# A gated attention and expert block: the operands of TensorE's turns declared float32r

## The reference

```python
def _L0_xattn_ref(p, k_v, W_k, b_k, ln_gamma, ln_beta):
    kv = k_v @ W_k.T + b_k
    out = jnp.einsum('bij,bjd->bid', p, kv)
    sim = jnp.einsum('bid,bjd->bij', out, kv) * scale
    # layer norm of sim over its last axis, with gamma and beta
    attn = jax.nn.softmax(sim, axis=-1)

def _L0_ffn_ref(x, gate_w, e_bias, Wu, Wd, Wsu, Wsd):
    logits = h @ gate_w
    scores = jax.nn.sigmoid(logits)
    # the 4 best of 32 experts, out of the 2 best of 4 groups; weights normalised, times 2.5
    up = jnp.einsum('th,ehi->tei', h, Wu)
    act = _relu2(up)
    routed = jnp.einsum('tei,te,eih->th', act, combine, Wd)
    shared = _relu2(h @ Wsu) @ Wsd
    out = (routed + shared).reshape(orig_shape)

x = x + jnp.tanh(g_xattn[0]) * _L0_xattn_ref(_layernorm(x), ctx_512, ...)
x = x + jnp.tanh(g_ffn[0]) * _L0_ffn_ref(_layernorm(x), ...)
```

## Time and profile before

| | us |
|---|---|
| median of 3 runs | 545.59 (545.41 to 546.27) |
| span of the profiled execution | 543.3 |
| TensorE busy with products and turns | 531.8, 98% of the span |
| weight loads busy | 434.4, 80% |
| VectorE busy | 412.1, 76% |
| ScalarE busy | 339.5, 62% |
| GpSimd busy | 190.0, 35% |

### The profile page before, as it was taken

One profiled execution on the slowest core, in us unless ns is written; L12 is line 12 of the kernel. 1 busy time (PEld: TensorE's weight loads), 2 busy tenths in 40 slices (PEclk: granted clock), 3 DMA queues, 4 the chain that ended last, 5 costly groups with the idle time before them and its releaser, 6 DMA issues.

```text
span 543.3 us, 11125 instructions
## 1 busy us (share of the span) xinstructions
PE 531.8 (98%) x3090; PEld 434.4 (80%) x3091; DVE 412.1 (76%) x906; ACT 339.5 (62%) x669; POOL 190.0 (35%) x194
## 2 busy tenths in 40 slices
PE   7999999999999999999999999999999999999997
PEld 4555776778788888999999999999999999986553
DVE  4799995494998958666787897777677575756997
ACT  4778673755327855677778787776777776753210
POOL 2110000000000032655657766666656566531000
PEclk9999999999999999999999999999999999999999
DMA  8931012006000024997887988788889778899998
GB/s 311 350 125 39 14 65 77 2 1 210 23 1 0 2 78 151 358 322 222 307 254 237 317 274 254 277 261 275 269 299 316 272 246 268 270 316 358 411 415 328
DMA packets 56393, 116.48 MB, mean 214 GB/s; under 512 B 5493, under 2 KB 24054, under 8 KB 55926
## 3 DMA queue, kind: packets, MB, share of 16 engines
q1 hardware_dynamic: 43200, 72.97, 40.8%
q0 software_dynamic: 12960, 42.48, 21.5%
q10 hardware_dynamic: 150, 0.07, 0.0%
HBM read 85.87 MB, written 29.62 MB: 213 GB/s over the span
## 4 chain that ended last, share of the span: by engine, by line
PE 73%; DVE 14%; DMA 5%; ACT 4%; issue 2%; SPq 1%; DVEq 0%; POOL 0%; ACTq 0%; POOLq 0%
PE U L1805 32%; PE D L1805 28%; PE T L2164 6%; DVE X L1782 5%; PE D L2183 3%; DMA yg<-y_rows 2%; PE T L1805 2%; SPq L508 1%; DVE X L1130 1%; DVE X L1184 1%; DMA y_rows<-yb,idx_s 1%; DVE bst L1135 1%; DMA h_rows<-HR 1%; DVE PS L1118 1%; PE T L1963 1%
## 5 line engine op out<-in xcount | busy, mean ns | idle before, releaser
L618 POOL DMA_INDIRECT xg<-h_rows,idx_g x81 | 88.0, 1086 | 107.9 <-DVE idx_g L1530 70.9
L625 POOL DMA_INDIRECT y_rows<-yb,idx_s x81 | 89.6, 1106 | 81.5 <-ACT yb L935 63.9
L1564 DVE TENSOR_TENSOR xgT_lo<-T,xgT_hi 128x512 fp32r<-128x512 f32 x81 | 56.0, 691 | 48.5 <-ACT xgT_hi L918 48.2
L935 ACT ACTIVATE yb<-D 128x512 f32<-128x512 f32 x81 | 48.7, 602 | 58.2 <-PE D L1805 58.2
L1805 PE MATMUL U<-wu_hi,xgT_hi 128*128 x324 | 58.2, 301 | 0.6 <-DVE xgT_lo L1564 0.6
L1805 PE MATMUL D<-wd_hi,eaT_hi 128*128 x162 | 57.3, 435 | 0.0
L918 ACT ACTIVATE xgT_hi<-T 128x512 fp32r<-128x512 f32 x81 | 48.1, 594 | 10.5 <-issue 8.7
L1805 PE MATMUL U<-wu_hi,xgT_lo 128*128 x324 | 51.8, 282 | 0.0
L1805 PE MATMUL U<-wu_lo,xgT_hi 128*128 x324 | 51.6, 281 | 0.0
L1805 PE MATMUL D<-wd_lo,eaT_hi 128*128 x162 | 50.6, 394 | 0.0
L1805 PE MATMUL D<-wd_hi,eaT_lo 128*128 x162 | 50.1, 391 | 0.0
(11 more groups left out here) (272 smaller groups left out, 1131.5 us busy)
## 6 DMA issues: line engine op xcount, KB each, us to landing
wu<-in_L_ffn_Wu SPq DMA_DIRECT2D x32, 512.0 KB, 5.0
wd<-in_L_ffn_Wd SPq DMA_DIRECT2D x32, 512.0 KB, 5.3
yg<-y_rows SPq DMA_DIRECT2D x18, 512.0 KB, 10.9
out<-X SPq DMA_DIRECT2D x16, 256.0 KB, 5.9
X<-in_x SPq DMA_DIRECT2D x3, 1024.0 KB, 11.4
h_rows<-HR SPq DMA_DIRECT2D x3, 1024.0 KB, 4.3
yg<-y_rows SPq DMA_DIRECT2D x3, 1024.0 KB, 12.2
wsu<-in_L_ffn_Wsu SPq DMA_DIRECT2D x2, 1024.0 KB, 8.7
```

The lines of the kernel that those rows point to most:

```text
L618: pool.indirect_dma_start(out=xg[:, u, :], out_offset=None, in_=h_dram[:, :], in_offset=bass.IndirectOffsetOnAxis(ap=idx_g[:, t:t + 1], ax ...
L625: pool.indirect_dma_start(out=y_dram[:, :], in_=yb[:, u, :], in_offset=None, out_offset=bass.IndirectOffsetOnAxis(ap=idx_s[:, t:t + 1], ax ...
L935: ac.activation(yb[:, t % UNROLL, :], D[2 + t % 2][:, :], ACT.Copy)\
L1564: ve.tensor_tensor(xgT_lo[:, t % 2, :, :], T[t % 2][:, :].rearrange("p (h n) -> p h n", h=HB), xgT_hi[:, t % 2, :, :].bitcast(f32), ALU.su ...
```

## The change

All turns of context rows, keys, X, HR, logits, gathered rows and activations read their data through a second name of the same bytes, declared float32r; the output in PSUM is written through a float32r view of the same bank, and the identity is a float32r copy of the old one. The second names are tiles that are allocated and freed just before the old one, so that both get the same address. GpSimd copies the identity, and TensorE waits for this copy once, ahead of its first turn. The turns of the key weights, the bias, the table of experts and the first positions stay fp32. No other instruction changes. The diff, with the other renamed tiles (`HR_r`, `lgT_r`, `key2_r`, `ctx_r`, `keyT_r`, `eact_r`) left out, which follow the pattern of `X_r` and `xg_r`:

```diff
+        with ExitStack() as turned:
+            X_r = turned.enter_context(nc.sbuf_tensor("X_r", [P, NT, H], f32r))
         X = sb("X", [P, NT, H])
...
         ident = sb("ident", [P, P])
+        ident_r = sb("ident_r", [P, P], f32r)
...
+            with ExitStack() as turned:
+                xg_r = at("xg_r", [P, UNROLL, H], turned, f32r)
             xg = at("xg", [P, UNROLL, H], early)
...
+        def keys_turned(b):
+            return key2_r[:, b, :] if b < 2 else keyT_r[:, :]
...
+            pool.wait_ge(s["pool_c"], 2)
+            pool.tensor_copy(ident_r[:, :], ident[:, :]).then_inc(s["pool_i"], 1)
             pool.memset(lower[:, :], 0.0).then_inc(c, 1)
...
             pe.wait_ge(s["pool_c"], 2)
+            pe.wait_ge(s["pool_i"], 1)
             pe.transpose(T[0][:, 0:DC], wk[:, :], ident[:, :]).then_inc(s["pe_wk"], 1)
...
+            def turn(o, bits):
+
+                return pe.transpose(o.bitcast(f32r), bits, ident_r[:, :])
...
-                    i_ = pe.transpose(ctx_bank(b)[:, j * P:(j + 1) * P], ctx_b[:, j, :], ident[:, :])
+                    i_ = turn(ctx_bank(b)[:, j * P:(j + 1) * P], ctx_r[:, j, :])
...
-                    i_ = pe.transpose(T[0][:, j * P:(j + 1) * P], keys_of(b)[:, j * P:(j + 1) * P], ident[:, :])
+                    i_ = turn(T[0][:, j * P:(j + 1) * P], keys_turned(b)[:, j * P:(j + 1) * P])
...
-                    pe.transpose(p_bank(0, j)[:, 0:P], X[:, 0, j * P:(j + 1) * P], ident[:, :])
+                    turn(p_bank(0, j)[:, 0:P], X_r[:, 0, j * P:(j + 1) * P])
...
-                    i_ = pe.transpose(p_bank(b, j)[:, it * P:(it + 1) * P], X[:, b * TPB + it, j * P:(j + 1) * P],
-                                      ident[:, :])
+                    i_ = turn(p_bank(b, j)[:, it * P:(it + 1) * P], X_r[:, b * TPB + it, j * P:(j + 1) * P])
...
-                    i_ = pe.transpose(h_bank(b, it)[:, h * P:(h + 1) * P], HR[:, it, h * P:(h + 1) * P], ident[:, :])
+                    i_ = turn(h_bank(b, it)[:, h * P:(h + 1) * P], HR_r[:, it, h * P:(h + 1) * P])
...
-                    i_ = pe.transpose(U[1][:, it * P:(it + 1) * P], lgT[:, it * P:(it + 1) * P], ident[:, :])
+                    i_ = turn(U[1][:, it * P:(it + 1) * P], lgT_r[:, it * P:(it + 1) * P])
...
-                    i_ = pe.transpose(T[t % 2][:, h * P:(h + 1) * P], xg[:, t % UNROLL, h * P:(h + 1) * P], ident[:, :])
+                    i_ = turn(T[t % 2][:, h * P:(h + 1) * P], xg_r[:, t % UNROLL, h * P:(h + 1) * P])
...
-                    i_ = pe.transpose(D[t % 2][:, k * P:(k + 1) * P], eact[:, t % 2, k * P:(k + 1) * P], ident[:, :])
+                    i_ = turn(D[t % 2][:, k * P:(k + 1) * P], eact_r[:, t % 2, k * P:(k + 1) * P])
```

More of the change, by code:

```diff
@@ L59, in block_kernel @@
             HR_lo = turned.enter_context(nc.sbuf_tensor("HR_lo", [P, TPB, H], f32r))
+        with ExitStack() as turned:
+            HR_r = turned.enter_context(nc.sbuf_tensor("HR_r", [P, TPB, H], f32r))
         HR = sb("HR", [P, TPB, H])
@@ L67, in block_kernel @@
             wsu_h4 = chosen_all.enter_context(nc.sbuf_tensor("wsu_h4", [P, 2, HB, P], f32r))
+        with ExitStack() as turned:
+            lgT_r = turned.enter_context(nc.sbuf_tensor("lgT_r", [P, SEQ], f32r))
         lgT = sb("lgT", [P, SEQ])
@@ L126, in block_kernel @@
                 out2 = at("out2", [DC, 2, SEQ], ramp)
+                with ExitStack() as turned:
+                    key2_r = at("key2_r", [DC, 2, SEQ], turned, f32r)
                 key2 = at("key2", [DC, 2, SEQ], ramp)
@@ L141, in block_kernel @@
             with ExitStack() as attention:
+                with ExitStack() as turned:
+                    ctx_r = at("ctx_r", [P, TPB, DC], turned, f32r)
                 ctx_b = at("ctx_b", [P, TPB, DC], attention)
                 ctxT = at("ctxT", [DC, SEQ], attention)
+                with ExitStack() as turned:
+                    keyT_r = at("keyT_r", [DC, SEQ], turned, f32r)
                 keyT = at("keyT", [DC, SEQ], attention)
@@ L215, in block_kernel @@
             erel = at("erel", [P, 2, INNER], early)
+            with ExitStack() as turned:
+                eact_r = at("eact_r", [P, 2, INNER], turned, f32r)
             eact = at("eact", [P, 2, INNER], early)
@@ L306, in block_kernel @@
         names = """d_x00 d_small d_gate d_tanh d_wk d_bk d_h d_out
-            pool_c pool_r dve_c dve_wh pe_bk pe_g act_bk act_th
+            pool_c pool_i pool_r dve_c dve_wh pe_bk pe_g act_bk act_th
             dve_v dve_u dve_z dve_e dve_x1 dve_h dve_ws dve_lo dve_sh dve_hT dve_lg dve_ch
```

## The result

| | before | after |
|---|---|---|
| median of 4 runs, same chip | 545.55 (545.41 to 546.27) | 539.16 (538.74 to 539.82) |
| ratio | | 0.9887 (0.9875 to 0.99) |
| span of the profiled execution | 543.3 | 536.9 |

The change makes the kernel 6.4 us faster, 1.2%. The direction was as forecast and the time lies in the range, but the forecast was 21.1 us.

A forecast was written before the change was run, and what follows sets the result against it. TensorE, gapless in the expert loop and nearly always busy from 60 to 200 us, was taken as the bound; 18.0 + 3.1 = 21.1 us off the 545.59 us median gave 524.5, range 512 to 546.5.

The forecast's parts named there:

- The identity sets the turn's pace: Each turn on TensorE: the moving fp32 identity costs two cycles a column; float32r brings the stream from 107 to 53 ns.
- Rival 1: Turns cost the same in float32r because all 32 bits are handed on; 545.6 us, chance 0.27.
- The load stays at 140: Weight load of each turn: remains 140 ns in float32r, not a product's 188, since the turn sets it, not the type.
- Rival 2: Slower: float32r turns load in 188 ns and stand 120 apart; 6.3 us lost, 551.9 us, chance 0.16.
- What is late next: Once the stream is short, the turn's load sets the distance: 72 ns from start to start in place of 109.
- The sum for the loop: Expert loop: 486 turns, each cheaper by 109 - 72 ns, all on TensorE's path, gain 18.0 us.
- wrong in its size: Sign of failure: the first products after the turns start later by what the turns gave; no size put on it.
- 60 to 200 us, 3.1: Stretch before the loop: 84 turns gain 37 ns each, 3.1 us taken whole, bounds 0 and 4.5.
- First 60 us: Start of the kernel: 92 turns, other chains set part of the pace, gain taken as 0, at most 4.9 us.
- Tail 0, new copy and wait hidden: Tail has no turns, cost 0; identity's copy on GpSimd and TensorE's wait hidden with 1.8 us to spare, else 0.3.
- Rival 3: Expert loop: turns get cheap but TensorE runs into VectorE or a transfer, giving back half; 535 us, chance 0.07.

The follow-up runs named there:

- r5: A probe kernel of its own, computing nothing of the reference: rows and groups of turns and products on TensorE; float32r turns 86 ns apart, fp32 109; no kernel time.
- r9: Changed kernel with only the first batch's turns in float32r, all others fp32; 547.11 us, ratio 1.004 to the kernel before.
- r1: Changed kernel plus a value-neutral mask on VectorE's waits for the weights' high halves; 550.3 us, ratio 0.9911 to the kernel before.
- r4: Changed kernel with the first batch's turns of context, keys and X in fp32 again; 549.51 us, ratio 0.9922 to the kernel before.
- r3: Changed kernel with float32r only for the front's turns, the expert loop's in fp32; 548.15 us, ratio 0.9882 to the kernel before.
- r2: Changed kernel with float32r only for the expert loop's turns, the front's in fp32; 550.14 us, ratio 0.991 to the kernel before.
- r11: Changed kernel with six turns in one group, first batch in fp32 and the last of four row turns in fp32; 535.9 us, ratio 0.9827.
- r7: Changed kernel with the four row turns placed singly behind the first four down products, in float32r; 552.8 us, ratio 1.0103 to the kernel before.

## Why the prediction was right, and where not

- **The identity sets the turn's pace: right.** The mean duration fell from 272 to 237 ns (rows) and 225 ns (activations), the nearest distances within a group are 57 to 65 ns, and with few loaded columns the row of turns runs at 60. Two cycles a column would be 107 ns, one is 53. Rival 1, the same price, falls. The reading that I had made of the Trainium skill, "FP8 and Floating Point Precision", "TensorE Precision Notes", was that a turn that keeps every byte can't go in one pass; the turn did go at one cycle a column, and that it keeps every byte is not measured by these runs.
- **The load stays at 140: right.** Rival 2, slower by a load of 188, falls.
- **What is late next, "188 - 68, the same 68 off a turn's 140 gives 72 ns": right in kind, wrong in size.** In groups of four the mean is 74, but only because the first distances are short; the steady distance is 86. The 68 had no ground: r5's products of 256 columns stand 118 ns apart with a load of 108 ns, against 120 with one of 192, so the load never held them, and 188 - 120 measured nothing. The Trainium skill, "TensorE: Matmul & The Clock Gate", "Back-to-back issue gap", whose 81 ns I had weighed and left, is nearer to the measured 86 than my 72.
- **The sum for the loop, "486 x (109 - 72) = 18.0 us, all on the path": the step that failed.** It prices a turn by its neighbour turns and never asks for the last turn of a group, whose neighbour is a product with a load of 188. There the distance, by ends, grew from 122 to 188 ns (232 to 300 at the down products), and that twice a tile: 0.15 us in the chain, against 0.24 that the turns gave. Measured are 0.090 us a tile, 15 ns a turn and not 37. From the first turn of rows to the last the loop is 6.9 us shorter (278.2 to 271.3), where 18.0 were due. The prediction had named this as what would make it wrong in its size ("if the first products after the turns start later by what the turns gave"), and put no price on it, though the price could be bounded from its own rows: a load of 188 behind a stream of 53.
- **60 to 200 us, 3.1: mis-sized by the same step.** From 60 us to the first turn of `xg` the changed kernel wins 1.2 us on the one before, but r9, whose turns there are fp32, wins 0.6 in the same stretch: the trace of the kernel before has a wait of 0.43 us for `HR` at 136.31 us that neither of the two has. So some 0.6 us are left for the 84 turns. Their groups are mostly four turns with products between them.
- **First 60 us, 0 and at most a gain: wrong in sign.** By 15 us the kernel after is 1.7 to 1.9 us behind, by the late rise of the clock; r9 timed it alone at 2.1 us. From 17 to 47 us it neither wins nor loses, so but for the clock the 0 was right. The bound was taken from zero upwards; the prediction read PEclk 1.00 as 2.4 GHz, and no row was asked at which level TensorE ran in the first microseconds.
- **Tail 0, new copy and wait hidden: right.** From the first product of the shared expert's last batch (`HR_hi`) to its last down product it is 49.25 us in both traces. TensorE's first turn waits for `wk` alone, at 3.74 us; the copy on GpSimd is over at 1.79:

```profile
1.50 0.29 POOL L586 CAST ident_r<-ident 128x128 fp32r<-128x128 f32 x1
...
3.74 0.48 PE L1832 MATMUL T<-ident,wk 128*128 128x128 f32 x1 [3.74 <-DMA wk<-in_L_xattn_W_k]
```

- **Rival 3, given back by VectorE or a transfer: not seen on the chip of the result.** The waits of TensorE in the loop are 1.0 us in all, against 0.6 before. The low half of rows comes 0.9 us before the up products that read it (303.85 + 0.69 = 304.54, against 305.43 in the chain), in the place of 1.1, as forecast. On the chip of r1 to r4 the loop does wait, and part of the gain may go there; no trace of the kernel before was taken on it, so how much is open.

The account: +1.9 by 15 us, -1.2 to the first turn of `xg`, -6.9 in the loop, 0 in the tail, which is -6.2 of the 6.4 us measured.

What stays open is why the clock rises later. It did so in five of six profiles whose first batch was turned in float32r (14.65 to 16.2 us), and in the sixth, r3, it rose at 10.8; in the seven with fp32 turns there it rose between 8.0 and 11.1 us. In the kernel before it rose amid the second group of turns of X; after, TensorE had by then done the same turns in shorter streams, and the clock rose only amid the attention's products. Which property of the turns counts was not tried. The Trainium skill, "TensorE: Matmul & The Clock Gate", "Part 4: PE-mode transpose", says that turns do not count for the clock as other work does. In r2 the clock rose at 11.1 us, after 2.3 us of nothing but fp32 turns, and kernels that differ in the type of these turns differ in the rise; both speak against it as a rule for fp32 turns, without refuting it, and nothing here shows it for float32r ones.

## What to carry to other kernels

A matmul's stream can be halved and its cost stay: ask what the next one loads, and price the last of a short group with the load of what stands behind it. Short matmuls pay in long groups, not one by one, and it can pay to leave the last of a group long (r11, with groups of six and the first batch left as it was: 9.1 us in the place of 6.4). What runs in the first microseconds can also change when TensorE's clock rises, so a cheaper operation there needs a bound on both sides.

## What the runs showed of the hardware

- A float32r turn streams at about one cycle a column: 58 to 60 ns start to start with up to 64 loaded columns (53 would be one cycle), 86 with 128; an fp32 turn 109 (r5).
- In the loops of before, after, r7 and r11 and in r5 no load starts before the matmul ahead of its own does. It mostly starts 1 to 3 ns after it, and within and behind groups of float32r turns 26 to 53 ns after it. Behind two or more such turns a load of 188 ns makes the product end 65 to 70 ns later than behind fp32 turns; a load of 108 doesn't (117 ns against 187 by ends).
- A float32r product that moves 128 columns stands at 111 ns with a load of 192, one that moves 256 at 120 with a load of 192 and at 118 with one of 108: a load's duration is no bound for the distance (r5).
- At 1.2 GHz, TensorE's lower level, the fp32 products of 512 columns are 853 ns apart, at 2.4 GHz 429, with PEclk at 1.00 in both; float32r turns at 1.2 GHz are 127 apart, fp32 ones 213.
